# Projections as high-low fp32r products and a re-laid order of one attention and routing step

## Chip, core and metric

One core of a Trainium2 chip runs the whole program. The metric is the device time of one execution in microseconds (us), the median of three runs.

## What is computed

Eight batches of 512 tokens, 256 wide, pass an adaLN block: modulation from `c`, linear attention with 16 heads of 16, then a top-2 mixture of 8 experts whose capacity is 512 tokens each. Cut to what matters here:

```python
h = _layernorm(x) * (1 + ca) + sa
q, k = elu(h @ Wq.T + bq) + 1, elu(h @ Wk.T + bk) + 1
v = h @ Wv.T + bv
# per chunk of 128 tokens, S the running sum of k^T v
num = mask(q @ k.T) @ v + q @ S
den = sum(q * cumsum(k))
x = x + ga * ((num / den) @ Wo.T + bo)
h = _layernorm(x) * (1 + cb) + sb
# top 2 of h @ embeddings.T, places by a cumulative count, capacity 512
x = x + gb * experts(h)
```

## The kernel before

**Steps.** The attention half is a software pipeline over the batches. `steps` calls on every engine a `step(early, front, attend, route)`, each argument being another batch: `early` is loaded and gets its statistics, `front` is transposed and projected, `attend` goes through the four chunks of attention, `route` is normalised again and sent to the experts' lists. The step with front batch 0 stands alone; with front 1 there is no `route`; fronts 3 to 6 run in a hardware loop of two steps; with front 7 there is no `early`. A `tail` finishes batches 6 and 7. Then the eight experts run as products of high and low parts in fp32r.

**What sets the order.** There is no scheduler: every engine has its queue of instructions written out by hand in its own `step`, and semaphores hold one engine for another. An engine executes in its queue's order, so whatever stands behind a waiting instruction waits too.

**The front.** `normalise_x` (ACT, L686) writes `xn`; `front_h` (PE, L941) turns it into two PSUM banks; ACT's `front_h` (L693) applies the modulation and writes `h1T`, 128x512 for each k of two. `project` (L947) makes one 128x512 half of q or k from two fp32 matmuls, `front_v` (L976) half of v from four of 256 columns. ACT (`exp_q`, `exp_k`, L699 and L702) and DVE (`q_max` L1423, `k_max` L1428) apply elu+1; `k_sum` (DVE, L1436) is the running sum; `q_times_kcum` (POOL, L549) and `front_den` (PE, L1001) give the denominators.

**The denominators' way.** ACT copies them to `den_sb`. SP writes them to DRAM (`spread_den`, L392) and reads them back spread over 128 partitions (L396). DVE inverts them (`invert_den`, L1443), the first thing in the next step. SP writes the result (`spread_rden`, L403), waits until it has landed, and reads it back for the heads with eight DMAs (L407). `normalise(attend, 0)` (DVE, L1460) waits for those eight.

**Attend.** For each chunk t: `scores` (PE, L1038) into the four banks of `quad`, `mask` (DVE, L1470) into `sT`, `numerator` (PE, L1058 and L1070), `update_state` (PE, L1085) and `keep_state` (DVE, L1479), `normalise` (DVE, L1460), `out_project` (PE, L1098), `residual` (DVE, L1488 and L1491). `x_and_bias` (POOL, L557 and L563) has put x plus the gated bias into `x1`. That buffer is used by every second batch, so it waits until `x1` of two batches before has been written out (`x1_out`).

**Route.** `mean2`, `norm2` (POOL), `normalise_x1` (ACT, L753), `route_h` (PE, L1115), `route_logits` (L1139), then on DVE `route_top`, `route_choose`, `route_slots`, `route_places`, `route_weights` (L1558, L1560), `keep_carry` and `route_lists` (L1610), with `route_counts` and `route_lists` (PE, L1167) between them. SP writes the token rows (L456, L459) when `row_on` says so, and `x1` to the output (L437).

**SP's waits.** `load_x(early)` (L374) overwrites the `x_sb` that `x_and_bias(attend)` reads:

```python
def load_x(b):
    wait(sp, S["xb_on"], b.n - 1)
```

and on POOL the sum waits with

```python
wait(gp, x1_out[b.p], 16 * b.h)
```

**Banks.** Transposed h, q, k, v, transposed k, denominators, logits, counts and lists share the two banks of `ring`; `numerator` and `out_project` share a third.

Of the kernel before, what the change touches and what calls it, by code (L numbers as in the profile page):

```python
# [28 lines left out]
P = 128  # L29
# [60 lines left out]
def adaln_kernel(nc, x, wqT, wkT, wvT, woT, biases, bo, embT, w1T, w2T, cT, wmod, out):  # L90
# [12 lines left out]
    with ctx:  # L103
# [7 lines left out]
        wq_sb, wk_sb, wv_sb, wo_sb = (sb(f"w{c}_sb", [P, KH, D]) for c in "qkvo")  # L111
# [107 lines left out]
        den_sb = first("den_sb", [HEADS, SEQ])  # L219
        xhat = first("xhat", [P, TILES, D])  # L220
# [18 lines left out]
        y_sb = x1  # L239

# [24 lines left out]

        def x1_bank(b):

            return ring[0] if is_last(b) else o_bank
# [5 lines left out]
        Q_ORDER, RH_ORDER = (1, 0), (1, 0)  # L274
        RH_BANK, V_BANK, KT_BANK = (ring[0], ring[1]), (ring[1], ring[0]), (ring[1], ring[0])
        LOGIT_BANK, COUNT_BANK, LIST_BANK = ring[0], ring[1], ring[1]
# [6 lines left out]
        def q_bank(b, k):  # L283
            return bank[2 + k] if is_first(b) else ring[0]

        def k_bank(b, k):
            return bank[4 + k] if is_first(b) else ring[1]

        def den_bank(b):
            return bank[2] if is_first(b) else ring[0]  # L290

        DEN_BANK = ring[0]
# [6 lines left out]
            h1T_on q_expd q_on k_expd k_on v_on k_tok_on  # L299
# [52 lines left out]
        def _(sp):  # L352
# [8 lines left out]
            def load_weights():  # L361
                sp.dma_start(bias_in[:, :, :], biases).then_inc(S["w_in"], 16)
                for to, of in ((wq_sb, wqT), (wk_sb, wkT), (wv_sb, wvT)):
                    sp.dma_start(to[:, :, :], of.rearrange("(k p) m -> p k m", p=P)).then_inc(S["w_in"], 16)
# [24 lines left out]
            def spread_den(b):  # L389

                sp.wait_ge(S["den_on"], b.n + 1)
                sp.dma_start(den_dram[b.n], den_sb[:, :]).then_inc(den_out, 16)  # L392
                sp.wait_ge(den_out, 16 * (b.n + 1))
# [5 lines left out]
            def spread_rden(b):  # L399


                sp.wait_ge(S["rden_on"], b.n + 1)
                sp.dma_start(rden_dram[b.n].rearrange("h (g t) -> (h g) t", g=P // HEADS), rden_flat[:, :])\  # L403
                    .then_inc(rden_out, 16)
                sp.wait_ge(rden_out, 16 * (b.n + 1))
# [16 lines left out]
            def step(early, front, attend, route):  # L422
                if attend:
                    spread_rden(attend)
                if early and isinstance(early.n, int) and early.n == 0:
                    load_x(early)
                    load_weights()
                    load_x(batch(0, 1))
                    load_wmod(1)
                    load_wmod(2)  # L430
                    load_later_weights()
                elif early and not (isinstance(early.n, int) and early.n == 1):
                    load_x(early)
                if route:

                    sp.wait_ge(S["x1_on"], TILES * (route.n + 1))
                    sp.dma_start(out_tiles[route.n], x1[route.p][:, :, :]).then_inc(x1_out[route.p], 16)  # L437
                if front:
                    if isinstance(front.n, int) and front.n == 0:
                        wait(sp, S["gate_on"], 4)  # L440
                        sp.dma_start(mod_dram, mod_sb[:, :, :].rearrange("b m d -> b (m d)"))\
                            .then_inc(S["mod_out"], 16)
                        wait(sp, S["mod_out"], 16)
                    load_ga(front)
                if attend:
                    load_mod(attend)
                if front and not is_last(front):
                    spread_den(front)
                if route:

                    sp.wait_ge(S["row_on"], 2 * (route.n + 1))
                    rows_h(route)
                    rows_gate(route)

# [46 lines left out]
        def _(gp):  # L501
# [43 lines left out]
            def q_times_kcum(b):  # L545
                for k in range(KH):

                    gp.wait_ge(S["kcum_on"], KH * b.n + k + 1)
# [49 lines left out]
            def step(early, front, attend, route):  # L598
                if attend:
                    x_and_bias(attend)  # L600
# [1220 lines left out]
```

## Time and profile before

| | |
|---|---|
| median of 3 runs | 482.13 us (481.46 to 483.08) |
| the profiled execution | 479.8 us |
| its span | 478.1 us |
| PE busy | 400.7 us, 84% |
| weight loads (PEld) busy | 285.4 us, 60% |
| DVE busy | 321.1 us, 67% |
| ACT busy | 193.6 us, 40% |
| POOL busy | 213.3 us, 45% |
| granted clock, mean | 0.957 |

The span runs from the first to the last instruction, and the execution's own time is 1.7 us longer. Busy is the union of the recorded intervals of an engine. Matmuls overlap in the records, so what one costs in a dense stretch is read from the distance between starts. One fp32 matmul leaves two records, an fp32r matmul one.

### The profile page before, as it was taken

The page shows a single profiled execution, that of the slowest core. Times are in us where ns is not written, and L with a number is a line of the kernel's source. Part 1 is how long each engine was busy: PE and PEld are TensorE (multiplying, and loading weights), DVE is VectorE, ACT ScalarE, POOL GpSimd, SP SyncE. Part 2 cuts the span into 40 slices and gives each one's busy share as a digit, 9 for nine tenths or more (in the row PEclk, how much of TensorE's full clock was granted, in tenths as well). Part 3 has the DMA queues.
Part 4 walks back from the last instruction along what each step waited for, and adds up shares of the span by engine and source line. Part 5 has one row for each costly group of instructions (what it writes and reads, how often), then busy time and mean ns, then how long its engine had stood idle before and what let it go on. Part 6 is the DMA issues. An engine that isn't in the chain of part 4 may idle for free.

```text
span 478.1 us, 9144 instructions
## 1 busy us (share of the span) xinstructions
PE 400.7 (84%) x3238; PEld 285.4 (60%) x3238; DVE 321.1 (67%) x857; ACT 193.6 (40%) x322; POOL 213.3 (45%) x231
## 2 busy tenths in 40 slices
PE   3898888898897897989989889697417999999981
PEld 0444555665565574565566568565315888888871
DVE  7274945778688768778777867986743666666640
ACT  1455235526625624533452661313403455445520
POOL 4123232191271354236219127062345688887454
PEclk9999999999999999999999999998557999999997
DMA  8102304102502500520440230136438488888333
GB/s 260 48 4 41 113 6 133 48 7 100 171 1 81 190 6 8 179 88 5 131 136 5 97 129 1 64 122 212 157 91 278 113 194 205 196 192 209 43 44 45
DMA packets 40338, 49.68 MB, mean 104 GB/s; under 512 B 5881, under 2 KB 32506, under 8 KB 40306
## 3 DMA queue, kind: packets, MB, share of 16 engines
q1 hardware_dynamic: 33138, 36.55, 24.0%
q0 software_dynamic: 7168, 12.72, 13.6%
q8 instruction: 18, 0.29, 0.3%
q14 instruction: 14, 0.11, 0.1%
HBM read 31.84 MB, written 17.42 MB: 103 GB/s over the span
## 4 chain that ended last, share of the span: by engine, by line
PE 67%; DVE 15%; ACT 9%; issue 5%; DMA 2%; POOL 1%; POOLq 0%; ACTq 0%; SPq 0%; DVEq 0%
PE bank L947 11%; PE bank L976 6%; PE quad L1038 5%; PE bank L1070 5%; PE bank L1273 4%; PE bank L1098 4%; PE quad L1273 3%; PE bank L1275 3%; PE bank L1274 3%; PE quad L1275 3%; PE quad L1274 3%; ACT xhat L753 3%; PE bank L1139 3%; PE bank L1058 2%; PE bank L1001 2%
## 5 line engine op out<-in xcount | busy, mean ns | idle before, releaser
L1470 DVE TENSOR_TENSOR sT<-quad,causal 128x1024 f32<-128x1024 f32 x64 | 75.1, 1215 | 13.3 <-PE quad L1038 13.3
L653 POOL DMA_INDIRECT out<-x,tok_i x32 | 52.6, 1643 | 25.2 <-DVE x L1767 18.5
L549 POOL TENSOR_TENSOR kcum<-qT,kcum 128x512 f32<-128x512 f32 x16 | 20.4, 1274 | 93.4 <-DVE kcum L1436 93.4
L1273 PE MATMUL bank<-w_hi,in_hi 128*128 128x256 f32 x128 | 37.0, 289 | 6.2 <-DVE in_lo L1752 6.2
L642 POOL DMA_INDIRECT xg<-token_rows,tok_i x32 | 32.9, 1028 | 19.0 <-issue 9.1
L1070 PE MATMUL bank<-sT,v_pad 128*32 128x128 f32 x1024 | 40.8, 278 | 0.0
L860 ACT ACTIVATE in_hi<-quad 128x512 fp32r<-128x512 f32 x32 | 19.1, 598 | 51.2 <-PE quad L1275 51.2
L1038 PE MATMUL quad<-q_bd,kT 32*128 32x256 f32 x512 | 37.5, 400 | 0.5 <-ACT q_bd L719 0.5
L1098 PE MATMUL bank<-wog,oT 128*128 128x256 f32 x128 | 33.9, 387 | 4.4 <-DVE oT L1460 4.4
L1752 DVE SCALAR_TENSOR_TENSOR in_lo<-quad,in_hi 128x512 fp32r<-128x512 f32 x32 | 22.1, 691 | 22.7 <-ACT in_hi L860 22.7
L1275 PE MATMUL bank<-w_lo,in_hi 128*128 128x256 f32 x128 | 36.2, 283 | 0.0
L1274 PE MATMUL bank<-w_hi,in_lo 128*128 128x256 f32 x128 | 36.2, 283 | 0.0
L976 PE MATMUL bank<-wv_sb,h1T 128*128 128x256 f32 x128 | 31.8, 391 | 1.4 <-DVE kT L1428 1.4
L1038 PEld LDWEIGHTS quad<-q_bd,kT 32*128 32x128 f32 x512 | 23.6, 184 | 12.3 <-issue 9.5
L947 PE MATMUL bank<-h1T,wk_sb 128*128 128x512 f32 x56 | 27.0, 604 | 3.4 <-ACT h2T L762 3.4
L1070 PEld LDWEIGHTS bank<-sT,v_pad 128*32 128x32 f32 x1024 | 25.8, 109 | 6.8
L1098 PEld LDWEIGHTS bank<-wog,oT 128*128 128x128 f32 x128 | 22.9, 190 | 11.0 <-DVE oT L1460 5.5
L1273 PEld LDWEIGHTS bank<-w_hi,in_hi 128*128 128x128 f32 x128 | 24.5, 191 | 8.3 <-issue 5.7
L1767 DVE SCALAR_TENSOR_TENSOR x<-bank,w_now,aside 128x256 f32<-128x256 f32 x32 | 15.4, 482 | 20.9 <-PE bank L1275 20.9
L726 ACT ACTIVATE v_pad<-bank 128x256 f32<-128x256 f32 x32 | 10.5, 381 | 46.2 <-PE bank L976 46.2
L947 PE MATMUL bank<-h1T,wq_sb 128*128 128x512 f32 x56 | 27.8, 618 | 1.5 <-ACT h1T L693 1.2
L1058 PE MATMUL bank<-qT,state 128*128 128x128 f32 x96 | 22.5, 316 | 6.3 <-DVE state L1479 6.3
(207 smaller groups left out, 923.4 us busy)
## 6 DMA issues: line engine op xcount, KB each, us to landing
token_rows<-h SPq DMA_DIRECT2D x8, 528.0 KB, 3.1
x_sb<-x SPq DMA_DIRECT2D x8, 512.0 KB, 4.0
out<-x SPq DMA_DIRECT2D x8, 512.0 KB, 5.0
token_rows<-mod_all SPq DMA_DIRECT2D x8, 512.0 KB, 4.2
w_sb<-w1T SPq DMA_DIRECT2D x8, 512.0 KB, 4.5
w_sb<-w2T SPq DMA_DIRECT2D x8, 512.0 KB, 4.7
rden<-rden_rows SPq DMA_DIRECT2D x56, 64.0 KB, 2.3
mod_all<-mod_rows SPq DMA_DIRECT2D x8, 384.0 KB, 5.3
```

The costliest lines, as they stand in the source:

```text
L642: gp.indirect_dma_start(out=xg[q][:, t, :], out_offset=None, in_=rows, in_offset=bass.IndirectOffsetOnAxis(ap=tok_i[:, 0, at:at + 1], axis=0),
L653: gp.indirect_dma_start(out=out_rows, out_offset=bass.IndirectOffsetOnAxis(ap=tok_i[:, 1, at:at + 1], axis=0), in_=y_sb[q][:, t, :], in_of ...
L947: last = mm(to[:, :], w[:, k, m * P:(m + 1) * P], h1T[:, k, :], start=(k == 0), stop=(k == KH - 1))
L976: last = mm(V_BANK[r][:, t * D:(t + 1) * D], h1T[:, k, tok(2 * r + t)], wv_sb[:, k, :], start=(k == 0), stop=(k == KH - 1))
L1038: last = mm(quad[:, r, k * 2 * P:(k + 1) * 2 * P].rearrange("p (s i) -> p s i", s=2), kT[b.p][at, k, tok(t)], q_bd[b.p][at, k, :, tok(t)], ...
L1058: mm(o_bank[:, k * P:(k + 1) * P], state[(t - 1) % 2][:, k, :], qT[b.p][:, k, tok(t)], start=True, stop=False, skip_group_check=True)
L1070: last = mm(o_bank[at:at + 32, k * P:(k + 1) * P], pair[:, 32 * (h % 2):32 * (h % 2) + 32], sT[t % 2][:, 4 * (h // 2) + 2 * k + h % 2, :], ...
L1098: last = mm(x1_bank(b)[:, 0:D], oT[t % 2][:, k, :], wog[:, k, :], start=(k == 0), stop=(k == KH - 1))
L1273: mm(out, a_hi, b_hi, start=first, stop=False)
L1274: mm(out, a_lo, b_hi, start=False, stop=False)
L1275: return mm(out, a_hi, b_lo, start=False, stop=last)
L1470: v.tensor_tensor(sT[t % 2][:, 8 * a:8 * (a + 1), :].rearrange("p (r s) i -> p r (s i)", s=2), quad[:, 2 * a:2 * a + 2, :].rearrange("p r ...
```

## The change

1. **Operands.** The weights of q, k and v are kept as `wqkv_hi` and `wqkv_lo` in fp32r, made once in the first step from a landing place in `rden` (ACT copies, DVE subtracts). h is kept as `h1_hi` and `h1_lo`: ACT writes `h1T` and, from the same bank, `h1_hi`; DVE's `low_h` writes the difference.
2. **Products.** A half of q or k is six fp32r matmuls of 512 columns instead of two in fp32, a half of v twelve of 256 columns instead of four.
3. **The step.** PE, ACT, DVE, POOL and SP get other orders, and the shared banks other tenants.
4. **The tail.** PE turns the last tile and makes its logits ahead of `route_lists(r)`.

```diff
-            def project(to, w, m):
-                for k in range(KH):
-                    last = mm(to[:, :], w[:, k, m * P:(m + 1) * P], h1T[:, k, :],
-                              start=(k == 0), stop=(k == KH - 1))
-                return last
+            def project(to, b, j, m):
...
+                pe.wait_ge(S["h1_hi_on"], KH * (b.n + 1))
+                part(wqkv_hi, h1_hi, first=True)
+                part(wqkv_lo, h1_hi)
+                pe.wait_ge(S["h1_lo_on"], KH * (b.n + 1))
+                return part(wqkv_hi, h1_lo, last=True)
```

```diff
+            def high_h(b, k):
+                modulate_h(h1_hi, "h1_hi_on", b, k)
...
+            def low_h(b, k):
+                dve.wait_ge(S["h1T_on"], KH * b.n + H1_ORDER.index(k) + 1)
+                dve.wait_ge(S["h1_hi_on"], KH * b.n + HI_ORDER.index(k) + 1)
+                v.tensor_tensor(h1_lo[:, k, :], h1T[:, k, :], full(h1_hi[:, k, :]), ALU.subtract)\
+                    .then_inc(S["h1_lo_on"], 1)
```

```diff
+                if early:
+                    load_x(early)
+                if front:
+                    load_ga(front)
+                if attend:
+                    rden_to_dram(attend)
+                    load_mod(attend)
+                    rden_to_heads(attend)
+                if front and not is_last(front):
+                    den_to_dram(front)
                 if route:
                     sp.wait_ge(S["row_on"], 2 * (route.n + 1))
                     rows_h(route)
                     rows_gate(route)
+                    x1_to_out(route)
+                if front and not is_last(front):
+                    den_by_rows(front)
```

**SP, the step with front 2**, whose order the loop steps share. L403 and L436 write the inverted denominators, L407 and L443 read them for the heads, L374 and L387 load x, L437 and L417 write x1 out. Before:

```order
L403 DMA rden_rows<-rden_flat 128x64 [waits rden_on]
L407 DMA rden<-rden_rows 16x2x512 [waits rden_out]
L407 DMA rden<-rden_rows 16x2x512 x7
L374 DMA x_sb<-x 128x4x256 [waits xb_on]
L437 DMA out<-x_0 128x4x256 [waits x1_on]
L379 DMA ga_all<-mod_rows 128x256 [waits wog_on]
L385 DMA mod_all<-mod_rows 128x768
L392 DMA den_rows<-den_sb 16x512 [waits den_on]
L396 DMA den_flat<-den_rows 128x64 [waits rden_on,den_out]
L456 DMA token_rows<-h 128x4x264 [waits row_on]
L459 DMA token_rows<-mod_all 128x4x256
```

and now:

```order
L387 DMA x_sb<-x 128x4x256 [waits xb_on]
L392 DMA ga_all<-mod_rows 128x256 [waits wog_on]
L436 DMA rden_rows<-rden_flat 128x64 [waits rden_on]
L398 DMA mod_all<-mod_rows 128x768
L443 DMA rden<-rden_rows 16x2x512 [waits rden_out]
L443 DMA rden<-rden_rows 16x2x512 x7
L405 DMA den_rows<-den_sb 16x512 [waits den_on]
L487 DMA token_rows<-h 128x4x264 [waits row_on]
L490 DMA token_rows<-mod_all 128x4x256
L417 DMA out<-x_0 128x4x256 [waits x1_on]
L411 DMA den_flat<-den_rows 128x64 [waits rden_on,den_out]
```

The loads of x, of ga and of mod moved ahead of the heads' reads, x1's write moved from the step's start to its end, and the spread read of the denominators moved behind the token rows and x1.

**DVE, the same step, from its start to the first `normalise`** (L1460, now L1544; `h_lo` is `h1_lo`). Before:

```order
L1443 RECIPROCAL rden_flat<-den_flat 128x64 [waits rden_out,den_in]
L1470 TENSOR_TENSOR sT<-quad,causal 128x1024 [waits sc_on,oT_mm]
...
L1479 TENSOR_TENSOR state<-bank,same_head 128x256 [waits oT_mm,kv_mm]
L1423 SCALAR_TENSOR_TENSOR qT<-bank,bias_p,q_exp 128x512 [waits q_expd]
...
L1428 SCALAR_TENSOR_TENSOR kT<-bank,bias_p,k_exp 128x512 [waits k_expd]
L1423 SCALAR_TENSOR_TENSOR qT<-bank,bias_p,q_exp 128x512 [waits q_expd]
L1436 SCALAR_TENSOR_TENSOR kcum<-ones,kT 128x512 [waits den_mm,k_on]
L1460 TENSOR_TENSOR oT<-bank,rden 128x256 [waits wo_mm,oT_mm,rden_in1]
```

and now:

```order
L1493 TENSOR_TENSOR h_lo<-h1T,h_hi 128x512 [waits h1_hi_on,h1T_on] x2
L1554 TENSOR_TENSOR sT<-quad,causal 128x1024 [waits sc_on,oT_mm]
L1554 TENSOR_TENSOR sT<-quad,causal 128x1024 [waits sc_on]
L1563 TENSOR_TENSOR state<-bank,same_head 128x256 [waits oT_mm,kv_mm]
L1584 BN_AGGR mv<-stat 128x2 [waits stats2]
L1584 BN_AGGR mv<-stat 128x2 x3
L1507 SCALAR_TENSOR_TENSOR qT<-bank,bias_p,q_exp 128x512 [waits q_expd]
L1512 SCALAR_TENSOR_TENSOR kT<-bank,bias_p,k_exp 128x512 [waits k_expd]
L1544 TENSOR_TENSOR oT<-bank,rden 128x256 [waits wo_mm,oT_mm,rden_in1]
L1499 BN_STATS stat<-x_sb 128x6 [waits x_in1]
```

The first `normalise` moved ahead of a q maximum and a running sum, and of `early_stats`, which all stand behind it now; the two `low_h` came in ahead of it.

## Rows read from the trace of the kernel before

**Rows 1.** Busy time in one loop step (stretch, engines, clock, DMA).
```profile
113.00:151.30 38.30, 34.41 (x316) 22.68 (x315) 29.60 (x90) 17.25 (x30) 15.74 (x20) 1.00 0.27 87
```
**Rows 2.** The chain that ended last: start, us; first `scores` of steps.
```profile
39.15 1.15 PE quad L1038 x16
...
74.81 1.08 PE quad L1038 x16
...
113.19 1.07 PE quad L1038 x16
...
268.09 1.08 PE quad L1038 x16
...
307.46 1.15 PE quad L1038 x16
```
**Rows 3.** PE's timeline in a loop step: start, us; projections and followers.
```profile
154.65 1.98 PE L947 MATMUL bank<-h1T,wq_sb 128*128 128x512 f32 x4
156.47 0.61 PE L1085 MATMUL bank<-v_pad,k_tok 128*128 128x128 f32 x4
...
171.25 1.97 PE L976 MATMUL bank<-wv_sb,h1T 128*128 128x256 f32 x8
173.06 0.39 PE L1058 MATMUL bank<-qT,state 128*128 128x128 f32 x2
```
**Rows 4.** PE's timeline in an expert, fp32r products of 256 and 512 columns.
```profile
387.08 0.28 PE L1274 MATMUL bank<-w_hi,in_lo 128*128 128x256 f32 x1
387.20 0.28 PE L1275 MATMUL bank<-w_lo,in_hi 128*128 128x256 f32 x1
...
390.08 0.40 PE L1274 MATMUL quad<-x_hi,w_lo 128*128 128x512 f32 x1
390.31 0.39 PE L1275 MATMUL quad<-x_lo,w_hi 128*128 128x512 f32 x1
```
**Rows 5.** ACT's modulation of h; min, median and max in ns.
```profile
L693 ACT ACTIVATE h1T<-bank,mod_T x16: 754/777/778, 14.5 to 269.8; 128x512 f32<-128x512 f32 x16
```
**Rows 6.** DVE's subtraction for the experts' x, from PSUM.
```profile
L1746 DVE TENSOR_TENSOR x_lo<-bank,x_hi x16: 680/686/692, 360.9 to 449.8; 128x512 fp32r<-128x512 f32 x16
```
**Rows 7.** DVE's groups in the step 113:151.3: busy, mean ns, idle before.
```profile
L1470 DVE TENSOR_TENSOR sT<-quad,causal 128x1024 f32<-128x1024 f32 x8 | 9.4, 1216 | 1.7 <-PE quad L1038 1.7
L1460 DVE TENSOR_TENSOR oT<-bank,rden 128x256 f32<-128x256 f32 x4 | 1.7, 416 | 1.2 <-PE bank L1070 1.2
L1428 DVE SCALAR_TENSOR_TENSOR kT<-bank,bias_p,k_exp 128x512 f32<-128x512 f32 x2 | 1.5, 746 | 2.6 <-ACT k_exp L702 2.6
```
**Rows 8.** SP's timeline at the start of a loop step.
```profile
190.69 0.41 SPq L456 DMA_DIRECT2D token_rows<-h  x1
191.28 0.41 SPq L459 DMA_DIRECT2D token_rows<-mod_all  x1
192.36 0.38 SPq L403 DMA_DIRECT2D rden_rows<-rden_flat  x1
195.57 4.07 SPq L407 DMA_DIRECT2D rden<-rden_rows  x8
199.91 0.39 SPq L374 DMA_DIRECT2D x_sb<-x  x1
```
**Rows 9.** DMA issues of the page: KB each, median us from issue to landing.
```profile
out<-x SPq DMA_DIRECT2D x8, 512.0 KB, 5.0
...
rden<-rden_rows SPq DMA_DIRECT2D x56, 64.0 KB, 2.3
mod_all<-mod_rows SPq DMA_DIRECT2D x8, 384.0 KB, 5.3
```
**Rows 10.** L403's answer: us from issue to landing, min, median, max.
```profile
DMA to landing us min/median/max: 1.5/3.5/3.7
```
**Rows 11.** POOL's timeline: the sum that frees x.
```profile
221.37 2.35 POOL L563 TENSOR_TENSOR x<-x_sb,bo_g 128x1024 f32<-128x1024 f32 x1
```
**Rows 12.** PE's timeline at the first projections, front batch 0.
```profile
16.14 3.78 PE L947 MATMUL quad<-h1T,wq_sb 128*128 128x512 f32 x4 [0.87 <-ACT h1T L693]
19.72 2.36 PE L947 MATMUL quad<-h1T,wk_sb 128*128 128x512 f32 x4
```
**Rows 13.** DVE's timeline in the tail, lists of batch 6, logits of 7.
```profile
338.55 0.26 DVE L1610 TENSOR_TENSOR lists<-bank,lists 128x96 f32<-128x96 f32 x1 [0.60 <-PE bank L1167]
340.92 0.19 DVE L1517 COPY logits<-quad 128x32 f32<-128x32 f32 x1 [2.12 <-PE quad L1130]
```

More of the change, by code:

```diff
@@ L219, in adaln_kernel @@
         den_sb = first("den_sb", [HEADS, SEQ])
+        h1_hi, h1_lo = (first(f"h1_{part}", [P, KH, SEQ], F32R) for part in ("hi", "lo"))
         xhat = first("xhat", [P, TILES, D])
@@ L608, in step @@
                     q_times_kcum(front)
-                if route:
-                    row_h(route, xhat)
-                if early and attend:
-                    norm1(early)
             def norm2_tiles(b, at, before):
@@ L802, in step @@
-                    spread_q(front)
-                if early and not (front and is_first(front)):
+                    front_v(front, 0)
+                    front_v(front, 1)
+                    front_kt(front, 1)
+                if early:
                     normalise_x(early)
+                if is_last(front):
+                    widen_rden()
             def widen_rden():
@@ L1180, in step @@
                 if front:
+                    wait(pe, S["k_tok_on"], 2 * front.n)
                     front_h(front, 1)
+                    if route:
+                        wait(pe, S["lists_on"], route.n)
+                    wait(pe, S["v_on"], 4 * front.n)
+                    front_h(front, 0)
                 if route:
                     out_project(route, 3)
-                if front:
-                    front_q(front, 1)
                 if attend:
                     update_state(attend, 0)
+                    scores(attend, 1)
@@ L1192, in step @@
                 if front:
+                    pe.wait_ge(S["q_on"], KH * front.n + 1)
+                    front_k(front, 1)
+                if attend:
+                    update_state(attend, 1)
+                    out_project(attend, 0)
+                if front:
+                    pe.wait_ge(S["k_on"], KH * front.n + 1)
                     front_q(front, 0)
                 if attend:
-                    update_state(attend, 1)
-                    numerator(attend, 0)
-                    scores(attend, 2)
+                    numerator(attend, 1)
@@ L1669, in step @@
                 if attend:
-                    mask(attend, 3)
                     normalise(attend, 2)
@@ L1674, in step @@
                 if route:
+                    route_weights(route, mark)
                     route_slots(route, mark)
```

479 lines of the change are left out of this document (264 added, 215 removed).

## The prediction

> **What bounds the kernel now.** I read the busy times by stretch first, then the chain that ended last, then PE's timeline of one loop step. In a loop step PE is busy 34.4 of 38.3 us, DVE 29.6, ACT 17.3, POOL 15.7, at full clock [rows 1]. The chain gives the lengths from one first `scores` to the next [rows 2]: 35.7 us with front 1, 38.4 with front 2, 154.9 for fronts 3 to 6, so 38.7 each, and 39.4 with front 7. The reader should see that PE has under 4 us of slack in a step and DVE under 9. PE is the bound, but what takes 3 us off PE leaves DVE nearly as tight, and DVE waits in order. So the sum is of steps, not of matmuls.
>
> **The products, on PE.** The start of the next work lies 1.82 us behind a half of q or k, and 1.81 behind a half of v [rows 3]. In the experts a 512-column fp32r matmul follows another after 0.23 us, a 256-column one after 0.12, each with its own weight load [rows 4]. Six of the first kind make 1.37 us, twelve of the second 1.44. Per batch: 4 x 0.45 + 2 x 0.37 = 2.5 us less, 20 us over eight batches, from PE alone. The Trainium skill (Perfetto Trace Analysis, Engine Utilization) halves the tensor peak for FP32_LOW_HIGH; if that were this fp32, two passes would cost 2 x 0.23 per matmul against 3 x 0.23 for the three products, and each half of q or k would get 0.46 us slower. The rows speak against it: two fp32 matmuls take 1.82 us, so one takes four passes of 0.23.
>
> **What it adds.** ACT writes h twice more: 2 x 0.78 us per batch [rows 5], beside 17.3 busy of 38, so it hides unless it stands between `front_h` and the first projection. There it does: four activations, 3.1 us, from the first transposed bank to the last. In PE's new order an `out_project`, an `update_state`, a `scores` and a `numerator` stand between, about 3.4 us. It is hidden; without that cover it would cost up to 1.5. DVE gets two subtractions of 128x512. The nearest row reads PSUM and takes 0.69 [rows 6]; back to back I take 0.65, so 1.3 per batch and 31 us of work for DVE. That the next work on PE must wait for `h1_lo` costs nothing while q's four first matmuls (0.9) run. In the first step three copies and three subtractions of the weights come in, some 0.6 each.
>
> **The order of a step, worked.** I laid the new order of every engine beside the durations of the old one. Time zero is the first `scores`. The last list of the old step ends on DVE at 0.6, the reciprocal at 1.2, the first mask at 3.5. Ahead of the first `normalise` stand two masks (4.7 [rows 7]), a reciprocal 0.55, a residual 0.85, `low_h` 1.3, a state 0.35, the aggregates 0.4, a q and a k maximum 1.4. With two short waits DVE would be at `normalise(attend, 0)` at 10.7. From there to the end of `route_weights` is 16.8: DVE's 29.6 plus 1.3, less the 9.6 ahead and 6.2 behind (slots 1.4, a residual 0.85, places 3.05, a normalise 0.35, carry and lists 0.6), and 1.7 for hand-overs. From `normalise(attend, 0)` to the next first `scores` is 22.6. PE's work between, with its waits, fits under that: the 2.6 us that `k_max` waits now [rows 7] and most of the other stalls go, since each bank's next tenant comes when DVE has passed. What is late next is the heads' reciprocals.
>
> **The reciprocals without a load ahead** (front 2, where no earlier x1 has to leave). Now the heads' reads begin 3.2 us after the write's issue, take 4.1 to issue, and the last lands 2.3 later [rows 8, 9]. From the end of the reciprocal that is 10.1; `normalise` starts at 11.3, the next `scores` at 33.9. I take 34.1 instead of 38.4: 4.3 less.
>
> **The loop steps.** Here the SP order makes a ring of waits that the old one did not have. `rden_to_dram` stands behind `load_x(early)`, which waits for POOL's sum in `x_and_bias(attend)`, which waits for the landing of x1 of two batches before; and that DMA is now issued at the end of the step before, behind the token rows. From the end of `route_weights`: 0.1 to the issue of the rows, 0.6 to the second [rows 8], 0.5 to x1's, landing 5.0 [rows 9], the sum 2.35 [rows 11], the issues of x and ga 1.4, the write of the reciprocals 3.5 [rows 10], the heads' issues 3.7 up to the last, its landing 2.3 [rows 9]. Together 19.4. With 16.8 back to `route_weights` the ring is 36.2 us long. Before it did not exist: the reads were out before x was asked for, and the sum ran at the end of the step before. So four steps gain 38.7 - 36.2 = 2.5 each, 10.0 in all, and the first `normalise` waits near 13.5 us after `scores` instead of 11.3. Bounds of the unknown: x1's landing behind 1 MB more than usual, 3.2 to 6.7; the write behind x and ga, 1.5 (alone [rows 10]) to 5.3 (as `load_mod` [rows 9]); the heads behind mod, 0 to 1.7 more. The ring then has 32.4 to 41.4 us; below 34 PE and DVE hold the step.
>
> **Front 1.** The ring is half there: `load_x(2)` waits for the first sum, which waits for ga. `normalise` comes at about 14.5, but without route the rest is only 18: 32.7 instead of 35.7, 3.0 less. **Front 7** has no load of x and no statistics: about 35.4 instead of 39.4, 4.0 less, PE's 31.5 and waits for the bound. **Front 0:** now the projections start at 16.1 at the half clock, the first half taking 3.6 us [rows 12]; the new first one waits for the weights' copies and both parts of h until 17.4, the four end at 24.9 instead of 25.4, v saves 0.7, the new wait for k's bank gives 0.2 back. 1.0 less. **Tail:** the logits' copy waits 2.1 us behind the lists [rows 13]. With the last tile turned and its logits made first, PE reaches the lists only about 1.2 later; of the 2.1 remain 0.9 less. The experts are unchanged.
>
> **Sum.** 1.0 + 3.0 + 4.3 + 10.0 + 4.0 + 0.9 = 23.2. The profiled execution took 479.8 (span 478.1 and 1.7 around it), so 456.6. The median of the runs lies 2.3 above that execution, which gives **459** as the time. About 0.3% (1.4 us) is what a measurement of this kernel can tell from no change.
>
> **Rivals.**
> *The ring is shorter* (landings near their lower ends), and PE and DVE hold all steps at some 34.1: four times 2.1 more, and a little in front 1, 449. For: the queue has few bytes in flight, the DMAs are busy 27% of a step [rows 1]. Against: 1.5 MB go out right then. Chance 0.17.
> *DVE becomes the bound.* 31 us of DVE work in a 36 us step leaves it almost no wait that can be absorbed; if a semaphore hold or a wait out of turn costs 2 us in each of the seven steps, 473. For: DVE's waits are in order. Against: its order leaves a pause before `normalise`. Chance 0.15.
> *Nothing is gained:* the ring at 40 us eats what PE gives (4 x 1.3 lost, and fronts 1, 2 and 7 gain less, the heads being late there too), 482. Chance 0.03.
> *Slower: the ring is much longer.* Of the 23.2, 13.2 come from outside the four loop steps. So the kernel is slower if the ring passes 38.7 + 3.3 = 42 us, 5.8 over my sum. It needs x1's write, x, ga and mod each to hold the small DMAs behind them for their full length, 2 us more than my upper terms. At 44 us: 4 x 5.3 - 13.2 = 8 more, 490. Chance 0.09.
> *fp32 has two passes,* the skill's halving: 0.46 x 4 and about 0.4 x 2 more on PE per batch, 2.6 x 8 = 21, 503. Rows 3 and 4 leave it 0.01.
>
> **How the numbers follow.** The forecast has 0.55. The range reaches to the short ring and nearly to the DVE case: 447 to 473. Faster 0.87, same 0.03, slower 0.10.
>
> **What would show it.** Records of L1010 0.23 us apart and of L1032 0.12. First `scores` 34.1 apart for front 2 and 36.2 in the loop. In the loop DVE idle for about 2 us before the first L1544, and SP issuing L436 some 2 us behind the end of the reciprocal, after L387; in front 2 without that. If the loop steps are as short as front 2's, the ring was wrong; if the stall is elsewhere on DVE, the hand-laid order was; if the spacing in L1010 is not 0.23, the products were.

## The result, and the profile after

The changed kernel takes 468.1 us (median of 4, 467.2 to 469.5) against 481.8 for the kernel before beside it (481.1 to 483.1): ratio 0.972, 95% interval 0.968 to 0.975. The gain is 13.7 us, the forecast was 23. The profiled execution took 468.5 (span 466.7). Here and in the table of experiments a median is of all runs of a kernel, while a ratio compares only the runs within 1.5% of their kernel's fastest, and is left out where a single run is left (e6, e10).

By stretch, from one first `scores` to the next, the changed kernel with fronts 1 to 7 (columns: stretch, length, busy PE, PEld, DVE, ACT, POOL, then granted clock, DMA share, GB/s):

```profile
39.25:75.52 36.27, 30.99 (x294) 22.29 (x295) 22.80 (x37) 13.92 (x24) 12.71 (x12) 0.95 0.19 56
75.52:109.62 34.10, 32.32 (x339) 25.16 (x336) 31.95 (x90) 19.41 (x34) 14.31 (x15) 1.00 0.28 89
109.62:147.91 38.29, 34.43 (x337) 26.43 (x335) 32.10 (x95) 18.46 (x32) 16.69 (x20) 0.96 0.28 85
147.91:185.38 37.47, 34.11 (x338) 26.21 (x336) 32.07 (x96) 18.46 (x32) 17.54 (x20) 0.95 0.28 88
185.38:223.16 37.78, 34.22 (x335) 26.20 (x335) 30.73 (x94) 18.46 (x32) 17.51 (x20) 0.95 0.28 89
223.16:260.16 37.00, 33.92 (x337) 26.25 (x335) 31.80 (x95) 18.46 (x32) 17.54 (x20) 0.95 0.28 86
260.16:295.03 34.87, 32.87 (x349) 26.65 (x348) 30.71 (x84) 16.88 (x28) 15.09 (x12) 1.00 0.26 79
```

Against [rows 1, 2]: front 2 is at the 34.1 of the forecast, and front 7 better by 0.5. The four loop steps together are 150.5 (before 154.9, forecast 144.8), front 1 is 36.3 (before 35.7, forecast 32.7). Front 0 is 39.25 instead of 38.15, and the tail with the experts 1.0 longer than before instead of 0.9 shorter. The clock, 1.00 in all these steps before, is 0.95 or 0.96 in five of seven.

The products have the spacing that was forecast [rows 3, 4], but a half costs more than its 1.37 us. PE's timeline of front 2, one half of q: the second and third pair of matmuls start 0.46 us apart, the first lies 0.66 ahead of the second, and the next work starts 1.58 behind the first. The other halves of that step take 1.50 or 1.51 (the other of q, both of k, the first of v) and 1.59 (the second of v). Per batch that is 9.2 us for six halves against 10.9 before, 1.7 less where 2.5 was forecast.

```profile
88.00 0.82 PE L1010 MATMUL bank<-h_hi,wqkv_hi 128*128 128x512 f32 x2
88.66 0.62 PE L1010 MATMUL bank<-h_hi,wqkv_lo 128*128 128x512 f32 x2
89.12 0.62 PE L1010 MATMUL bank<-h_lo,wqkv_hi 128*128 128x512 f32 x2
89.58 0.38 PE L1105 MATMUL bank<-qT,state 128*128 128x128 f32 x2
```

The ring is there too. The timeline of the loop step that begins at 147.91, in order of time over the engines (start, us), from the end of `route_weights` (L1644) of the step before:

```profile
142.15 0.19 DVE L1644 TENSOR_TENSOR h<-weighted 128x32 f32<-128x32 f32 x1
...
148.96 2.37 POOL L595 TENSOR_TENSOR x<-x_sb,bo_g 128x1024 f32<-128x1024 f32 x1 [13.52 <-DMA out<-x]
149.01 0.55 DVE L1527 RECIPROCAL rden_flat<-den_flat 128x64 f32<-128x64 f32 x1 [0.73 <-DMA den_flat<-den_rows]
...
151.50 0.40 SPq L387 DMA_DIRECT2D x_sb<-x  x1
...
152.60 0.38 SPq L436 DMA_DIRECT2D rden_rows<-rden_flat  x1
...
156.17 3.87 SPq L443 DMA_DIRECT2D rden<-rden_rows  x8
...
161.96 0.42 DVE L1544 TENSOR_TENSOR oT<-bank,rden 128x256 f32<-128x256 f32 x1 [2.79 <-DMA rden<-rden_rows]
162.44 1.55 PE L1145 MATMUL bank<-wog,oT 128*128 128x256 f32 x4 [2.33 <-DVE oT L1544]
163.43 1.41 PE L1010 MATMUL bank<-h_hi,wqkv_hi 128*128 128x512 f32 x2
164.01 2.37 POOL L626 TENSOR_TENSOR h<-h,mod_all 128x1024 f32<-128x1024 f32 x1
164.64 1.05 PE L1010 MATMUL bank<-h_hi,wqkv_lo 128*128 128x512 f32 x2
164.90 2.57 DVE L1520 TENSOR_TENSOR_SCAN kcum<-ones,kT 128x512 f32<-128x512 f32 x1
165.49 1.05 PE L1010 MATMUL bank<-h_lo,wqkv_hi 128*128 128x512 f32 x2
```

POOL waits for x1's landing, SP asks for x when the sum is done and only then writes the reciprocals, which had been ready since 149.6. `normalise` comes 14.05 behind `scores` (forecast near 13.5). Three things were not in the forecast. The reciprocal waits 0.73 for the landing of `den_flat`; it is still done 3 us before its write is issued, so this wait is not part of the ring. Behind the stall PE's pairs of matmuls stand 0.85 apart instead of 0.46, at the lower of the clock's two levels. And the running sum L1520 takes 2.57 us; it ends 1.1 behind POOL's L626, and takes 1.2 where no POOL instruction runs beside it. DVE is not idle once from 161.96 to the last list at 185.17.

### The profile page after: what moved, and what is told of

It is laid out like the page before. It is cut to its first block, busy times and chain, and to the rows that moved or that the text cites. A ratio compares the mean times of both kernels' runs of the same rounds, so it can differ in the third digit from the quotient of the medians.

```text
span 466.7 us, 9558 instructions
## 1 busy us (share of the span) xinstructions
PE 391.6 (84%) x3366; PEld 307.4 (66%) x3366; DVE 334.7 (72%) x876; ACT 204.7 (44%) x341; POOL 225.4 (48%) x231
## 4 chain that ended last, share of the span: by engine, by line
PE 39%; DVE 20%; issue 16%; POOL 8%; DMA 8%; ACT 4%; SPq 3%; POOLq 1%; DVEq 0%; ACTq 0%
DVE sT L1554 6%; PE bank L1345 4%; PE quad L1345 3%; PE bank L1347 3%; PE bank L1346 3%; PE quad L1347 3%; PE quad L1346 3%; PE quad L1085 3%; PE bank L1010 2%; PE bank L1117 2%; DMA rden_rows<-rden_flat 2%; DMA out<-x 2%; PE bank L1145 2%; DVE kcum L1520 2%; SPq L443 2%
## 5 line engine op out<-in xcount | busy, mean ns | idle before, releaser
L595 POOL TENSOR_TENSOR x<-x_sb,bo_g 128x1024 f32<-128x1024 f32 x8 | 18.9, 2363 | 76.2 <-DMA out<-x 76.0
L1085 PE MATMUL quad<-q_bd,kT 32*128 32x256 f32 x512 | 42.7, 403 | 6.9 <-DVE sT L1554 5.4
L1145 PE MATMUL bank<-wog,oT 128*128 128x256 f32 x128 | 36.2, 407 | 10.3 <-DVE oT L1544 10.3
L1085 PEld LDWEIGHTS quad<-q_bd,kT 32*128 32x128 f32 x512 | 26.8, 184 | 15.3 <-DVE sT L1554 8.1
L1347 PE MATMUL bank<-w_lo,in_hi 128*128 128x256 f32 x128 | 36.2, 283 | 0.0
L1346 PE MATMUL bank<-w_hi,in_lo 128*128 128x256 f32 x128 | 36.2, 283 | 0.0
L1145 PEld LDWEIGHTS bank<-wog,oT 128*128 128x128 f32 x128 | 22.5, 196 | 13.5 <-DVE oT L1544 11.3
L581 POOL TENSOR_TENSOR kcum<-qT,kcum 128x512 f32<-128x512 f32 x16 | 21.9, 1382 | 15.6 <-DVE kcum L1520 15.0
L740 ACT ACTIVATE q_exp<-bank,neg_b 128x512 f32<-128x512 f32 x14 | 9.6, 688 | 43.9 <-PE bank L1010 43.9
L1520 DVE TENSOR_TENSOR_SCAN kcum<-ones,kT 128x512 f32<-128x512 f32 x16 | 28.5, 1785 | 0.0
L1345 PE MATMUL quad<-x_hi,w_hi 128*128 128x512 f32 x64 | 25.9, 405 | 1.8 <-DVE x_lo L1838 1.8
L1346 PE MATMUL quad<-x_hi,w_lo 128*128 128x512 f32 x64 | 25.6, 399 | 0.0
```

The costliest lines, as they stand in the source:

```text
L581: gp.tensor_tensor(qk[:, k, :], qT[b.p][:, k, :], kcum[:, k, :], ALU.mult)\
L1085: last = mm(quad[:, r, k * 2 * P:(k + 1) * 2 * P].rearrange("p (s i) -> p s i", s=2), kT[b.p][at, k, tok(t)], q_bd[b.p][at, k, :, tok(t)], ...
L1145: last = mm(x1_bank(b)[:, 0:D], oT[t % 2][:, k, :], wog[:, k, :], start=(k == 0), stop=(k == KH - 1))
L1345: mm(out, a_hi, b_hi, start=first, stop=False)
L1346: mm(out, a_lo, b_hi, start=False, stop=False)
L1347: return mm(out, a_hi, b_lo, start=False, stop=last)
```

## The experiments

The theory after these rows: the ring is the bound of a loop step; cut it, and the step goes to some 34. The rivals: DVE's queue behind `normalise` is the bound anyway, or PE's load is. Lengths below come from each run's profiled execution, in us; "rest" is the tail and the experts. The medians are of 5 or 6 runs (changed 4, e7 11).

| kernel | front 0 | 1 | 2 | 3 to 6, sum | 7 | rest | profiled | median (range) | ratio to before, 95% |
|---|---|---|---|---|---|---|---|---|---|
| before | 39.2 | 35.7 | 38.4 | 154.9 | 39.4 | 170.6 | 479.8 | | |
| changed | 39.3 | 36.3 | 34.1 | 150.5 | 34.9 | 171.7 | 468.5 | 468.1 (467.2 to 469.5) | .968 to .975 |
| e1 | 38.4 | 35.6 | 34.5 | 142.6 | 35.7 | 171.4 | 459.9 | 465.5 (459.9 to 467.7) | .959 to .969 |
| e2 | 38.6 | 35.5 | 34.1 | 141.1 | 34.8 | 172.6 | 458.3 | 460.3 (458.3 to 465.6) | .952 to .964 |
| e3 | 38.9 | 34.9 | 33.6 | 149.5 | 34.7 | 173.1 | 466.4 | 466.4 (465.0 to 469.4) | .964 to .974 |
| e4 | 39.4 | 34.5 | 36.1 | 146.9 | 36.3 | 172.3 | 467.3 | 466.4 (466.3 to 469.3) | .964 to .972 |
| e5 | 38.1 | 37.6 | 33.3 | 139.7 | 34.0 | 173.3 | 457.7 | 457.7 (453.5 to 468.7) | .940 to .952 |
| e6 | 38.1 | 37.6 | 33.3 | 138.7 | 41.0 | 171.7 | 462.1 | 462.2 (455.0 to 464.9) | none |
| e7 | 41.1 | 38.8 | 35.1 | 152.8 | 35.1 | 171.5 | 476.1 | 480.2 (476.1 to 487.8) | .993 to .999 |
| e8 | 36.5 | 39.5 | 35.1 | 154.0 | 37.6 | 173.0 | 477.3 | 473.9 (469.3 to 477.3) | .976 to .986 |
| e9 | 39.5 | 33.1 | 33.3 | 147.6 | 34.9 | 171.5 | 461.6 | 459.9 (455.1 to 465.0) | .943 to .953 |
| e10 | 39.0 | 34.9 | 33.5 | 138.9 | 41.2 | 173.6 | 462.8 | 462.2 (453.7 to 467.0) | none |
| e11 | 42.3 | 35.4 | 35.0 | 140.3 | 35.8 | 171.5 | 461.9 | 464.6 (461.9 to 466.0) | .960 to .968 |
| e12 | 38.6 | 34.9 | 33.8 | 141.3 | 41.6 | 173.7 | 465.6 | 456.9 (450.7 to 465.6) | .938 to .949 |

**e1: x1 leaves early.** On SP `x1_to_out(route)` stands behind `rden_to_heads(attend)`.

```diff
                     rden_to_heads(attend)
+                if route:
+                    x1_to_out(route)
...
                     rows_gate(route)
-                    x1_to_out(route)
```

> SP issues x1_to_out(route) right behind rden_to_heads, no longer behind the token rows; nothing else differs from the changed kernel (468.1). Theory (the ring): POOL's L595 then waits for no landing at the head of a loop step, SP's load_x no longer holds the write of the reciprocals, the first normalise comes at 11.3 to 11.6 us behind the first scores instead of 14.05, and with that wait gone PE's clock stays at its upper level. The four loop steps go from 37.6 to 34.3 or 34.5 us, as front 2's 34.1 without the ring; 4 x 3.1 = 12.5 less, 455.6. Rival 1 (the work behind normalise, not the wait before it, holds the step, since DVE is idle nowhere else): the step stays within 1 us of 37.6, 464 or more. Rival 2 (a transfer that moves collides): x1's write now runs beside the heads' reads, which land late again, 462.

**e2: the reciprocals ahead of x.** x1 leaves late, as in the changed kernel.

```diff
-                if early:
-                    load_x(early)
-                if front:
-                    load_ga(front)
                 if attend:
                     rden_to_dram(attend)
                     load_mod(attend)
                     rden_to_heads(attend)
+                if early:
+                    load_x(early)
+                if front:
+                    load_ga(front)
```

> SP issues the write of the reciprocals, mod and the heads' reads ahead of load_x and load_ga; x1 still leaves behind the token rows. Theory (the ring is closed by load_x standing ahead of rden_to_dram): the ring is cut here too, at its other end. normalise at 11.3 behind scores; but x is now asked for at 9.5 us and DVE's early_stats wants it at 11.7, so a new DVE wait of 1 to 2 us stands there: loop steps 35.3, front 1 half a us shorter than 36.3, total 459. Rival (x1's late landing hurts by itself, not by way of load_x): the loop steps stay at 37 to 38 and the total at 467 to 469.

Measured: `normalise` at 10.9 (e1) and 11.2 (e2) behind `scores` with no wait for a DMA, and loop steps of 35.6 and 35.3 on average, 7.9 and 9.4 us less in sum. Two edits at two ends of the ring do the same, and e2 still sends x1 out behind the token rows: the late landing hurt by way of `load_x` alone. The DVE wait for x that e2 was to bring came in one loop step of four, with 0.58 us. The steps stayed 1.3 us above the 34.3 expected of e1. In both profiles the first running sum of a step is long, 3.05 to 3.18 us in e1 and 2.39 to 3.12 in e2; e5 tests below whether that is the cause. Two rows of e1's loop step, DVE and POOL:

```profile
157.62 3.18 DVE L1521 TENSOR_TENSOR_SCAN kcum<-ones,kT 128x512 f32<-128x512 f32 x1
159.80 3.15 POOL L627 TENSOR_TENSOR h<-h,mod_all 128x1024 f32<-128x1024 f32 x1
```

Now that `normalise` is early, the sum meets POOL's `row_h` from the beginning (its first multiply runs 157.34 to 159.72): it waits, and then POOL's second waits for it.

**e3: POOL's order.** `row_h(route)` behind `q_times_kcum(front)`, which waits for both sums. **e4** is e1 and e3 together.

```diff
                     norm2(route)
-                    row_h(route, xhat)
                 if early:
                     norm1(early)
                 if front:
                     q_times_kcum(front)
+                if route:
+                    row_h(route, xhat)
```

> POOL runs row_h behind q_times_kcum instead of behind norm2, and q_times_kcum waits for both running sums. The ring stays. Theory (DVE's scan L1520 is long when a POOL tensor_tensor runs beside it: 2.57 us for 1.21): every scan takes 1.2 us, so what lies between normalise and the end of route_weights gets 1.3 us shorter in each of seven steps, and the ring with it: 468.1 - 7 x 1.2 = 459.7 at best, 461 with some of it taken by POOL's later end. Rival (scans vary for another reason, or the time is slack): scans stay at 1.6 on average and the total at 468; a second rival, row_h ends after route_weights and delays the token rows: above 468.

> Both edits of the runs on x1's place and on POOL's order. If the two causes are separate the gains add: 12.5 + 8 = 20.5, 448, loop steps of 33.2. If both only free the same wait, it comes out at the better of the two, about 455. If PE is the next bound (31.5 busy and its waits), 451.

Measured: all sixteen sums take 1.21 us in e3, as expected, and yet the total is 466.4 and the loop steps gain 0.25 each. What the sums gave up, 1.3 us per step, other instructions of DVE took: `gap` (L1614) takes 0.86 instead of 0.14 and the cast of `top_i` (L1624) 0.63 instead of 0.16 in every loop step, 1.2 together. e4's loop steps are even 1.1 us longer than e1's. Four rows of one of them show a third such instruction:

```profile
207.13 2.36 POOL L626 TENSOR_TENSOR h<-h,mod_all 128x1024 f32<-128x1024 f32 x1
209.59 0.63 DVE L1625 CAST top_f<-top_i 128x8 f32<-128x8 uint32 x1
210.27 2.42 POOL L595 TENSOR_TENSOR x<-x_sb,bo_g 128x1024 f32<-128x1024 f32 x1
210.40 2.32 DVE L1631 TENSOR_SCALAR wsum<-e 128x4 f32<-128x4 f32 x1
```

A `tensor_scalar` on four elements per partition, 0.16 us elsewhere, takes 2.32 and ends with POOL's L595; in the loop step of 147.55 it is the `tensor_tensor` behind it, 2.00 for 0.16. POOL instructions that the sums were spared now hold others of DVE's, and these stand in front of `route_weights`. One rival stands for e4: its loop steps have a granted clock of 0.91 to 0.95, e1's 1.00 in three of four, and how the 1.1 us divide between the waits and the clock was not separated. Masks, maxima and `bn_stats`, which read PSUM or one SBUF operand, show their usual length beside POOL. The Trainium skill (SBUF — State Buffer, Who interferes with whom) has such a rule: DVE and GpSimd share one pair of ports, the one that comes second blocks for the other's whole instruction, and DVE's copy, cast and `tensor_scalar` in their fast modes and its instructions with two SBUF inputs are concerned. The rows agree in each case seen here.

**e5: e2, and DVE's first sum ahead of `early_stats`.** **e6: also `den_by_rows` ahead of `x1_to_out` on SP.**

```diff
                     normalise(attend, 0)
+                if front:
+                    k_sum(front, 0)
                 if early:
                     early_stats(early)
```

```diff
                     rows_gate(route)
-                    x1_to_out(route)
                 if front and not is_last(front):
                     den_by_rows(front)
+                if route:
+                    x1_to_out(route)
```

> The run with the reciprocals ahead of x (460.3, steps of 35.2 in the loop), and on DVE the first running sum k_sum(front, 0) directly behind normalise(attend, 0), ahead of early_stats. In that run the sum began 0.3 us after POOL's row_h and took 3.12 us instead of 1.21. Theory (a running sum waits for the POOL tensor_tensor in flight): it now begins 2 us ahead of row_h and takes 1.2; DVE had no idle time behind normalise, so each step with a route gets 1.0 to 1.9 us shorter, loop steps 33.3 to 34.3, total 452. Rival 1 (PE with 32.8 busy of 35.2 is next): steps 34.8, total 457. Rival 2 (POOL's row_h holds the next instruction of DVE's instead, whatever it is): bn_stats grows from 0.35 each and nothing is gained.

> As the run with the first sum moved, and SP issues den_by_rows ahead of x1_to_out. DVE waits 0.75 us at the head of a loop step for den_flat, which goes out 0.1 us behind 0.5 MB of x1. Theory (the small read is held up by the big write ahead of it): the wait goes, 0.75 us in each of five or six steps, 4 less than that run, 448. Rival (the read is late because SP issues it late, behind row_on, whatever stands ahead): the wait shrinks by under 0.3 us and the total by under 1.5.

Measured in e5 (rows of DVE and POOL in one loop step): the first sum is out ahead of `row_h`, the second still meets its end.

```profile
191.47 1.22 DVE L1520 TENSOR_TENSOR_SCAN kcum<-ones,kT 128x512 f32<-128x512 f32 x1
193.58 2.37 POOL L622 TENSOR_TENSOR h<-xhat,mod_all 128x1024 f32<-128x1024 f32 x1 [2.40 <-ACT xhat L793]
196.03 2.36 POOL L626 TENSOR_TENSOR h<-h,mod_all 128x1024 f32<-128x1024 f32 x1
197.31 2.16 DVE L1520 TENSOR_TENSOR_SCAN kcum<-ones,kT 128x512 f32<-128x512 f32 x1
```

The three loop steps at full clock take 34.6, 34.1 and 34.4, the remaining one 36.6 at a clock of 0.95. In e6 DVE's wait for `den_flat` goes from 9.1 us in all to 3.9, the 3.9 being front 1's. Most of that is the rival's doing: the read is issued 1.0 us earlier behind `route_weights`, while its way from issue to landing only goes from 4.2 to 3.8 (medians). And the steps are no shorter for it: 34.2, 34.8, 34.1 and 35.6 (clock 0.95), as in e5. At full clock a step has come to the 34.1 that the forecast gave steps without a ring. But the medians, 457.7 and 462.2, lie above the expectations of 452 and 448. In e6's front 7 (stretch as above) the clock is low:

```profile
247.72:288.72 41.00, 38.82 (x349) 31.62 (x348) 32.60 (x84) 16.87 (x28) 16.67 (x13) 0.83 0.25 76
```

Where it falls is seen best in e9, a later run with the same order in the loop, all of whose loop steps have a lowered clock. PE's timeline there:

```profile
160.03 0.60 PE L1041 MATMUL bank<-ident,kT 128*128 128x128 f32 x4
160.47 1.89 PE L1177 MATMUL bank<-emb_sb,h2T 128*128 128x8 f32 x16
162.29 2.45 PE L1086 MATMUL quad<-q_bd,kT 32*128 32x256 f32 x16
164.67 0.80 PE L1106 MATMUL bank<-qT,state 128*128 128x128 f32 x2
```

and at the same place in a step of e6 whose clock stayed at 1.00:

```profile
128.56 1.89 PE L1177 MATMUL bank<-emb_sb,h2T 128*128 128x8 f32 x16
130.38 1.37 PE L1086 MATMUL quad<-q_bd,kT 32*128 32x256 f32 x16
131.68 0.49 PE L1106 MATMUL bank<-qT,state 128*128 128x128 f32 x2
```

From the fourth `scores` (L1086) on, e9's matmuls take 1.6 times as long (L1106 0.80 instead of 0.49), at the lower of the two levels. No idle time stands ahead of the fall, only transposes of 128 columns, an `out_project`, and sixteen logits matmuls of 8 columns. The same work stands ahead of that place in both steps, so it goes with the fall but does not settle it. The times of runs go with the clock too: e5's took 453.5 us at a mean clock of 0.947 and 457.4 and 457.7 at 0.934; e9's took 455.1 at 0.941, 457.3 at 0.930, 458.3 at 0.926 and 461.6 at 0.915.

**e7: eight matmuls for six, e8: four.** In the changed kernel, `part(wqkv_hi, h1_hi)` done twice, or `part(wqkv_lo, h1_hi)` left out; v likewise.

```diff
+                part(wqkv_hi, h1_hi, first=True, last=True)
                 part(wqkv_hi, h1_hi, first=True)
-                part(wqkv_lo, h1_hi)
```

(the + line is e7, the - line e8)

> The changed kernel (468.1) with its first two matmuls of each half of q and k done twice (eight of 512 columns, 1.84 us, the time of the old fp32 pair 1.82) and v likewise (16 of 256 columns): the new order with PE's old load, 2.8 us more per batch. If the products' time is what brought the gain, and the ring is what is left over, then fronts 2 and 7 and front 0 get about 2 us longer each, front 1 1.5, the loop steps, which the ring holds at 37.6, 1 each: 468 + 11 = 479. If the new order alone brought the gain (PE has slack): 468 to 470. If PE sets every step: 468 + 8 x 2.8 = 490, slower than before.

> The changed kernel without the product of the weights' low part and h's high part (left out of q, k and v, so the output is less exact): four matmuls of 512 columns per half, 2.8 us less per batch on PE. Theory (steps are held by the ring in the loop, and by DVE's queue in fronts 2 and 7): the loop steps stay within 0.7 us of 37.6, fronts 2 and 7 within 1 of 34, total 463 to 467, most of it from front 0 and front 1. Rival (PE is still the bound): 8 x 2.8 less, 446.

Measured: e7 480.2, as its first expectation had it (479). So 2.8 us of PE work per batch are worth some 12 us of time in the new order. That is not quite the share of the products in the 13.7: e7's halves take 1.97 to 2.06, more than the 1.82 of the kernel before, so it has 1.0 us more PE work per batch than that one, and is still 0.1 to 0.7% faster. New products in the old order were not run, so how the gain divides between products and order is known only roughly. e8 went against every expectation: 2.8 us less PE work per batch made it *slower* than the changed kernel, by 1.0% of the time before (4.6 us), with disjoint intervals. Two of its loop steps, and one of e7's:

```profile
147.88:191.00 43.12, 36.11 (x322) 26.02 (x320) 31.90 (x96) 18.35 (x32) 16.71 (x20) 0.84 0.25 79
...
227.92:265.07 37.15, 30.80 (x322) 22.94 (x320) 31.84 (x95) 18.35 (x32) 17.53 (x20) 1.00 0.29 87
```

```profile
153.08:191.94 38.86, 35.80 (x354) 27.58 (x352) 31.50 (x96) 18.58 (x33) 17.54 (x20) 1.00 0.27 86
```

At full clock e8's step is 37.15, that of the changed kernel less 0.4: there PE is not the bound, the ring is. At a clock of 0.84 it is 43. e8's runs have mean clocks of 0.897 to 0.914, the changed kernel's 0.927 to 0.935, so the loss goes with the clock; no run took the work away and kept the clock up. e7's clock is 1.00 in all loop steps.

**e9: e6, and two edits on DVE, one in front 1 and one in the tail.** **e10:** e9 and four matmuls of no use ahead of `route_lists`, where PE idles. **e11:** e9 with eight matmuls for six. **e12:** e9 and two such matmuls ahead of `route_logits`.

```diff
+                if attend and not route:
+                    mask(attend, 0)
+                    invert_den(attend)
...
                         keep_logits(b)
                         route_top(b)
+                        route_lists(r)
...
+                    for i in range(4):
+                        mm(kv_bank[:, :], wqkv_hi[:, 0, i % 2, 0:P], h1_hi[:, i % 2, :],
+                           start=True, stop=True, skip_group_check=True)
                     pe.wait_ge(S["v_on"], 4 * front.n + 4)
                     route_lists(route)
...
+                    for i in range(2):
+                        mm(ring[1][:, :], wqkv_hi[:, 0, i, 0:P], h1_hi[:, i, :],
+                           start=True, stop=True, skip_group_check=True)
                     route_logits(route)
```

(the first loop is e10's, the second e12's)

> As the run with den_by_rows ahead of x1_to_out, and two edits in stretches of their own, each read from its stretch. (a) Step with front 1 alone: DVE runs mask(attend, 0) ahead of invert_den(attend). There the reciprocal waited 3.9 us for den_flat and the first mask behind it, and PE idled 2.2 us for the mask. Theory (a wait at the head of DVE's queue costs what is queued behind it): the second scores starts 2.5 us earlier, front 1 takes 35.5 to 36 instead of 37.6, and PE's clock does not fall there. Rival (den_flat holds the step by way of normalise, wherever the reciprocal stands): front 1 stays at 37.6. (b) Tail: DVE copies and ranks the last batch's logits ahead of route_lists(r). Theory (the new PE order had the logits ready 0.9 us earlier, DVE stood behind the lists, and gap L1614 then waited for POOL's L626 to end): the logits' copy comes at 32.6 behind the last scores instead of 33.4, gap still has to wait for the end of L626, so 1 to 2 us less from the last scores to the first gather (45.3 now). Rival: PE's route_lists, now waited for later, takes the gain. Total 2 to 4 us under that run at equal clock, 452.

> As the run with front 1 and the tail mended, and PE does four matmuls of 512 columns on fp32r operands of its own (0.93 us, their result used by nobody) into the bank of the state, in each step with a route, ahead of route_lists, where it idled 0.8 to 0.9 us. Theory (what is lost beyond DVE's queue is lost where PE's clock goes to its lower level after stretches with little work, and work in a pause costs nothing): fewer of the steps show a granted clock under 1.00, the runs scatter less, the median is the same or up to 3 us lower. Rival (the clock falls for another reason): as many low steps as without. Rival 2 (the pause was needed: PE comes 0.1 to 0.9 late to route_lists, and so to the next scores): 3 to 5 us more.

> As the run with front 1 and the tail mended, with eight matmuls for six (PE's old load, 2.8 us more per batch). In the changed kernel this cost 11 to 12 us in all. If without the ring PE is the bound of a step: 34.2 + 2.8, loop steps near 36.5, total 470 to 474, or 18 to 20 above its base. If DVE's queue is the bound at some 34 and PE had slack: steps of 35, total 460. Either way the granted clock should be 1.00 in the loop steps, as it was with eight products before.

> As the run with front 1 and the tail mended (459.9), and PE does two matmuls of 512 columns on fp32r operands (0.47 us, their result used by nobody) into the logits' bank just ahead of route_logits. In that run's profile the granted clock fell in each of the four loop steps at the fourth scores, right behind the stretch with the transposes of xhat and k and the 16 logits matmuls of 8 columns; where it did not fall (other runs of the same order) the step took 34.2. Theory (it is the work PE does in that stretch that decides): with 0.47 us more there, fewer steps fall, at most one of six; loop steps 34.4, total 455 to 457. Rival 1 (only more load over the whole step helps, as with eight matmuls per half): the same number of steps fall, 460 to 462. Rival 2 (the work is in PE's way, falls or not): steps of 34.7 at full clock.

e9, front 1 and one loop step:

```profile
39.49:72.57 33.08, 29.57 (x294) 21.15 (x294) 23.48 (x37) 14.03 (x24) 12.71 (x12) 1.00 0.21 55
...
178.64:216.51 37.87, 36.21 (x336) 26.68 (x336) 32.53 (x93) 18.36 (x32) 17.80 (x20) 0.91 0.29 90
```

Front 1 goes from 37.6 to 33.1, more than expected: with mask and reciprocal in the other order PE gets its `scores(1)` and projections at once, and its clock stays up. In the tail the last logits are copied 32.6 behind the last `scores`, as expected, and still the first gather comes at 45.0 instead of 45.3:

```profile
322.32 2.35 POOL L627 TENSOR_TENSOR h<-h,mod_all 128x1024 f32<-128x1024 f32 x1
322.39 2.32 DVE L1625 CAST top_f<-top_i 128x8 f32<-128x8 uint32 x1
```

The time won ahead of POOL's instruction was spent waiting for it. All four of e9's loop steps have a lowered clock; that is 8.9 us over e6's in sum. The fillers settle little. e10's PE work in the pause costs nothing (its steps are e6's), and the clock falls in the same steps as in e6 (its front 7 takes 41.2): its rival, that the clock falls for another reason than this pause, stands. e12 has two steps of 38.3 and 41.6 at a fallen clock among seven; its median is the lowest of all, but its interval overlaps those of e5 and e9. e11 is clearer: with 2.8 us more PE work per batch every loop step is 34.9 to 35.3 at full clock, 0.9 above the best and 1.8 below e9's mean. Its total, 464.6, lies between its two expectations (460 with slack on PE, 470 to 474 with PE as the bound): PE is now 34.8 busy of 35.1, and had slack under the 34.2 of the other order. It is slower than e9 all the same, by 1.6% of the time before with disjoint intervals: fronts 0, 1, 2 and 7 got 0.9 to 2.8 us longer each. Its runs lie within 4.1 us, e9's within 10.

## Why the prediction was right, and where it missed

The time lies in the range and on the forecast's side, and the gain is 9.5 us short. By its steps:

- **The products**: the four passes and the 0.23 us between matmuls were right, and with them the rival of two passes is out. The price of a half was not: 1.50 to 1.59 us instead of 1.37 and 1.44, since the first pair starts 0.57 to 0.66 ahead of the second instead of 0.46 (v likewise). They save 1.7 us per batch, not 2.5, some 14 us of PE work in all instead of 20. The forecast was summed from steps, not from PE's work, so this does not show in its terms.
- **Front 2 and front 7**: 34.1 and 34.9 for 34.1 and 35.4. In front 2 some of it was luck: `normalise` came at 10.9 instead of 11.3, and from there it took 23.2 instead of 22.6. "What is late next is the heads' reciprocals" held in the loop only.
- **The ring**: right in each link, too short in two terms. From the end of `route_weights` to `normalise` the four loop steps take 20.3, 19.6, 20.6 and 19.6 us, forecast 19.4; the two longer ones have longer issues on SP (5.15 for the heads' eight instead of 3.87, and 1.72 for the second of the token rows instead of 0.40). "From there to the end of `route_weights` is 16.8" is the larger miss: it took 18.1, 17.5, 17.4 and 17.6. The running sums took 1.3 us per step more than the old trace had them; without that the term would have been too long by 0.4. In the old order they hardly met a `tensor_tensor` of POOL's (mean 1.25 us over sixteen, now 1.79). Together the four steps came out at 37.6 on average instead of 36.2, 5.7 us in all, with `normalise` at 13.9 to 14.7 instead of 13.5. The fallen clock is not the reason: in e3, at full clock, the first part takes 19.4 to 20.5 in the same steps.
- **The rivals**: the first, a shorter ring and all steps at 34.1, named the right floor. e5 and e6 reach it by cutting the ring and sparing one sum the wait for POOL. The ring alone takes 9.4 us of the change's gain in the loop (e2). The second, DVE as the bound through a hold or a wait out of turn, came half true: DVE is not idle behind `normalise`, and its waits for POOL are what lengthens that part.
- **Front 1**: "`normalise` comes at about 14.5" was near (15.0), "but without route the rest is only 18" was not: 36.3 instead of 32.7. The first mask waits behind a reciprocal that waits 4.2 us for `den_flat`, and with q and k now behind `scores(1)` PE had nothing else to do. The reciprocal waited 3.9 in the old order too, but there projections of PE stood beside the wait. e9, which takes the mask first, has 33.1.
- **Front 0**: 1.1 over the forecast in this profile, 38.1 to 39.5 in the others of the same front; the three longest, this one among them, have a granted clock of 0.87, but the two shortest have 0.91 and the others 1.00, so the clock does not explain the order. Why it missed the forecast stays open.
- **Tail**: the logits were ready 0.9 earlier, as forecast, but DVE stood behind `route_lists(r)`, and its next instruction with two SBUF operands behind POOL, as the timeline of DVE and POOL has it (before: [rows 13]):

```profile
328.29 0.26 DVE L1694 TENSOR_TENSOR lists<-bank,lists 128x96 f32<-128x96 f32 x1 [2.67 <-PE bank L1199]
328.46 0.18 DVE L1601 COPY logits<-quad 128x32 f32<-128x32 f32 x1
...
329.19 2.34 POOL L626 TENSOR_TENSOR h<-h,mod_all 128x1024 f32<-128x1024 f32 x1
...
329.65 1.90 DVE L1614 TENSOR_TENSOR gap<-top 128x4 f32<-128x4 f32 x1
```

  `gap` ends at 331.55, POOL's L626 at 331.53. Before, the same pair met too, and `gap` took 0.79. The difference, 1.1, is about what the tail grew by.
- **The clock**: no step of the forecast asked what PE's clock does when PE has less to do. In the changed kernel it cost little, because DVE had no idle time behind `normalise`: e3's loop steps at 1.00 still take 36.9 to 37.4. In the faster versions it is most of what is left: a loop step takes 34.1 to 34.8 at full clock (e5, e6) and 35.4 to 37.9 in e9.

What stays open: what makes the clock fall in one step and not in the next with the same work, and which matmuls would keep it up at least cost. e12 is one guess with two falls; that the place matters more than the amount is not shown.

## What to carry to other kernels

When an order is moved, follow each queue round until it closes: a small DMA behind a load that waits for a write of the step before can make a ring that no busy share shows, and undoing either end is one moved line. A duration from the old trace is that of the old neighbours. Before work is taken from PE, ask what its clock does in the stretch that is left with little in it.

## What the runs showed of the hardware

- DVE instructions with two SBUF operands, and casts and `tensor_scalar`s on SBUF, wait to the end of the POOL `tensor_tensor` in flight: 0.16 us became 2.32 (e4), 1.21 became 3.18 (e1), and POOL's 2.37 became 3.15 the other way round. A DVE instruction on four elements per partition waits as one on 512 does.
- PE's granted clock went to its lower level without any idle time ahead of it (e9, 162.29), behind transposes of 128 columns and matmuls of 8. Taking 2.8 us of matmuls per batch away lost 1.0% (e8); adding them to the order without a ring cost 1.6%, kept the clock at 1.00 in the loop, and the runs lay within 4.1 us instead of 10 (e11).
- The 32 KB read of `den_flat` lands 1.8 us behind its issue in the old order (median), where SP issues it ahead of the token rows; 3.8 behind the 1 MB of token rows (e6); and 4.2 behind the token rows and the 512 KB of x1 (e5).
